# Sending the reciprocal denominators of half the heads through device memory, and folding the values in one pass

## The chip, the cores and the metric

One core of one Trainium2 chip runs the whole program. The metric is the device time of one execution in microseconds. TensorE (PE) multiplies matrices into PSUM, VectorE (DVE) and ScalarE (ACT) do elementwise work and can read PSUM, GpSimd (POOL) does elementwise work between tiles of SBUF, and SyncE (SP) here does nothing but issue DMA transfers. Each engine runs its own list of instructions in order and waits on semaphores for the others.

## The reference

The input is a batch of 32 images of 56 x 56 pixels with 32 channels. Each passes through three stages, and each stage adds to its input:

1. group norm, batch norm, a sign function, and a 3x3 convolution with binary weights;
2. layer norm and a linear attention with 16 heads of 32 columns, over the 3136 pixels of an image;
3. layer norm, and a mixture of 8 linear experts of which each token uses the best two.

The change lies in the attention. For each token `s` and head `h`, cut to what matters:

```
q = elu(x wq + b) + 1 ; k = elu(x wk + b) + 1
kv_c = sum_s k cos(s) v ,  kv_s = sum_s k sin(s) v         (32 x 32 for each head)
ksum_c = sum_s k cos(s) ,  ksum_s = sum_s k sin(s)         (32 for each head)
denom = 1 / (q cos(s) . ksum_c + q sin(s) . ksum_s + 1e-5) (one number for each token and head)
out   = (q cos(s) . kv_c + q sin(s) . kv_s) * denom, then the dense layer
```

## The kernel before

**Tiling.** An image is cut into 7 tiles of 448 tokens (4 patches of 112). The 512 columns of q are 4 chunks of 128, each with 4 heads, so `qbuf` is [128, 4 chunks, 7 tiles, 448]. Work on an image is cut into some 100 steps with two-letter names, `K0` to `K13` and so on. Those that matter here are:

- `K` (L572, L713, L991): two patches of k. PE multiplies, ACT takes the exponential (L716), DVE combines them (L994). `KX` (L578) multiplies the result by the normed input, into a bank of PSUM of its own, and `KT` (L723) copies that out once for an image. `Q` (L598, L718, L997) is the same for q, in 14 steps, without the last part.
- `G` (L589, L726), in two steps: PE multiplies `ktsb` by the folded value and output weights `p2`. ACT copies the products to `gmat` (L729) and, with 8 tiny activations of 32 x 2 elements in each step, the key sums to the diagonal blocks of `dmat` (L734), whose other elements were set to zero once (L871).
- `DN` (L604, L1003), `SU` (L615, L736): denominators of a half image (4 or 3 tiles). `RC` (L1010, L740): DVE takes the reciprocal in `den`, ACT makes its half-precision part; `RL` (L1013): DVE makes the remainder. Both parts lie in `rs`.
- `R` and `RP` (L621), 7 steps each: two matmuls with the 0/1 matrix `sel16` spread the reciprocals of a tile over the 128 partitions, for chunks 0 and 1 (`R`) or 2 and 3 (`RP`). In `R`, DVE multiplies `qbuf` by the result straight from PSUM (L1022). In `RP`, ACT copies it to `spread_r` (L751), of which there is one buffer, and POOL multiplies (L815).
- `NM` (L630, L1024): the scaled q times `gmat`, one step for each tile. `T2`, `S2`, `SM2`, `PN2`, `XH2`, `PL2`, `ZU`, `LG`, `RT`, `GT`, `F`, `OUT`: the second layer norm, the router (`RT`, L1033 to L1077), the gates, the experts and the sum.
- `SM1`, `PN1`, `XH1`, `PL1`, `CS`, `ZT`: the first layer norm and the transposes that `K` and `Q` read. `PN1` and `PN2` are a power on POOL (L793) and a product (L797).

**PSUM.** Three slots of two banks go round (the ring) among the steps in `RING`, in PE's order. PE fills a slot only when its user three steps back has been read. One bank serves the steps in `MISC` in turn. An image has 57 uses of the ring: K 14, Q 14, R 7, RP 7, F 7, G 2, ZT 2, ZU 2, LG 1, XC 1.

**Order.** `schedule()` (L137) gives each step a time by hand, in units of which 14 make a period. `SHIFTS` (L190) moves a kind of step on one engine. `iteration()` (L203) folds the times modulo 14 and sorts, so each engine works in each period on three to five images at different stages, in one fixed order. Images 3 to 28 are done by a loop whose body holds two periods (L257), the others by straight code ahead of it and after it. The times set only the order: nothing waits for a clock.

**DMA.** SP loads an image (L474, 4 transfers, at `XT`), makes four shifted copies for the convolution (L488, 4 transfers of many short rows, at `CV`), and stores the result (L493, 4 transfers, at `OUT`).

## Time and profile before

| | |
|---|---|
| time, 3 runs | median 2821.83 us (2802.16, 2821.83, 2821.9) |
| profiled execution | span 2819.6 us; the median lies 2.2 us above it |
| PE busy | 2421.4 us, 86% |
| DVE busy | 2342.6 us, 83% |
| POOL busy | 1866.9 us, 66% |
| ACT busy | 1724.8 us, 61% |
| mean granted TensorE clock | 0.929 of full speed |

A profile is one execution. The profiled execution's own time is its span and the little that lies around it (start and end of the program); the page gives the span alone. Busy time is the time in which an engine executes; time in which an instruction is blocked on a shared resource counts as busy.

### The profile page before, as it was taken

The page shows a single profiled execution, that of the slowest core. Times are in us where ns is not written, and L with a number is a line of the kernel's source. Part 1 is how long each engine was busy: PE and PEld are TensorE (multiplying, and loading weights), DVE is VectorE, ACT ScalarE, POOL GpSimd, SP SyncE. Part 2 cuts the span into 40 slices and gives each one's busy share as a digit, 9 for nine tenths or more (in the row PEclk, how much of TensorE's full clock was granted, in tenths as well). Part 3 has the DMA queues.
Part 4 walks back from the last instruction along what each step waited for, and adds up shares of the span by engine and source line. Part 5 has one row for each costly group of instructions (what it writes and reads, how often), then busy time and mean ns, then how long its engine had stood idle before and what let it go on. Part 6 is the DMA issues. An engine that isn't in the chain of part 4 may idle for free.

```text
span 2819.6 us, 56945 instructions
## 1 busy us (share of the span) xinstructions
PE 2421.4 (86%) x19300; PEld 1207.1 (43%) x19300; DVE 2342.6 (83%) x3041; ACT 1724.8 (61%) x2821; POOL 1866.9 (66%) x1479
## 2 busy tenths in 40 slices
PE   3379999898989999898999989899998989999872
PEld 3324444444444444444444444444444444444442
DVE  4457999898988889898898989888898988899873
ACT  0057766666666666666666666666666666666640
POOL 0124677777767667776776777676677767777677
PEclk7579999999999999999999999999999999999995
DMA  9100000000000000000000000000000100000000
GB/s 249 35 10 10 10 16 16 16 6 12 16 17 16 16 16 11 7 16 17 16 16 16 14 4 16 17 16 16 17 15 2 16 17 16 16 10 7 7 7 12
DMA packets 232233, 55.14 MB, mean 20 GB/s; under 512 B 226065, under 2 KB 226945, under 8 KB 231777
## 3 DMA queue, kind: packets, MB, share of 16 engines
q1 hardware_dynamic: 231904, 50.95, 9.1%
q8 instruction: 184, 3.01, 0.5%
q14 instruction: 145, 1.18, 0.1%
HBM read 31.19 MB, written 12.85 MB: 16 GB/s over the span
## 4 chain that ended last, share of the span: by engine, by line
PE 40%; DVE 22%; POOL 17%; issue 14%; ACT 3%; DMA 1%; SPq 1%; POOLq 0%; DVEq 0%; ACTq 0%
PE ps L585 10%; PE ps L576 5%; PE ps L610 5%; DVE kbuf L994 5%; POOL prod L844 5%; DVE qbuf L1000 5%; PE ps L627 4%; PE ps L636 3%; POOL prod L847 3%; DVE rs L1017 2%; DVE route L1064 2%; POOL rstd L793 2%; PE ps L601 2%; ACT ebuf L716 2%; PE ps L568 2%
## 5 line engine op out<-in xcount | busy, mean ns | idle before, releaser
L716 ACT ACTIVATE ebuf<-ps,small 112x1024 f32<-112x1024 f32 x448 | 498.6, 1113 | 384.7 <-PE ps L576 357.3
L994 DVE SCALAR_TENSOR_TENSOR kbuf<-ps,ebuf 112x1024 f32<-112x1024 f32 x448 | 546.8, 1221 | 129.4 <-ACT ebuf L716 112.0
L721 ACT ACTIVATE ebuf<-ps,small 128x896 f32<-128x896 f32 x448 | 450.1, 1005 | 317.7 <-PE ps L601 237.8
L815 POOL TENSOR_TENSOR qbuf<-spread_r,qbuf 128x896 f32<-128x896 f32 x224 | 468.2, 2090 | 141.0 <-ACT spread_r L751 140.8
L585 PE MATMUL ps<-kbuf,xcs 112*64 112x512 f32 x1792 | 506.3, 651 | 45.1 <-DVE kbuf L994 45.1
L1000 DVE SCALAR_TENSOR_TENSOR qbuf<-ps,ebuf 128x896 f32<-128x896 f32 x448 | 486.3, 1085 | 37.6 <-ACT ebuf L721 35.3
L793 POOL TENSOR_TENSOR rstd<-varr,power 112x28 f32<-112x28 f32 x64 | 307.2, 4801 | 292.7 <-DVE varr L984 290.7
L636 PE MATMUL ps<-qbuf,gmat 128*64 128x224 f32 x3584 | 403.2, 369 | 4.5 <-DVE pbuf L1028 1.7
L844 POOL TENSOR_TENSOR prod<-prod 112x512 f32<-112x512 f32 x224 | 285.3, 1274 | 159.0 <-DVE prod L1084 157.9
L1084 DVE TENSOR_TENSOR prod<-ps,gate 112x1024 f32<-112x1024 f32 x224 | 272.4, 1217 | 94.4 <-PE ps L661 79.9
L627 PE MATMUL ps<-rs,sel 128*128 128x448 f16 x896 | 249.4, 360 | 96.6 <-issue 81.7
L576 PE MATMUL ps<-wk,z 128*112 128x512 f16 x896 | 287.7, 404 | 25.5 <-DVE qbuf L1000 17.9
L636 PEld LDWEIGHTS ps<-qbuf,gmat 128*64 128x64 f32 x3584 | 243.4, 140 | 129.0 <-issue 31.8
L601 PE MATMUL ps<-z,wq 128*128 128x448 f16 x896 | 248.6, 360 | 10.3 <-DVE qbuf L1000 8.3
L1022 DVE TENSOR_TENSOR qbuf<-ps,qbuf 128x896 f32<-128x896 f32 x224 | 242.4, 1082 | 12.4 <-PE ps L627 12.1
L751 ACT ACTIVATE spread_r<-ps 128x896 f32<-128x896 f32 x224 | 205.0, 915 | 63.0 <-PE ps L627 57.9
L610 PE MATMUL ps<-qbuf,dmat 128*32 128x448 f32 x1792 | 225.5, 549 | 0.2 <-ACT mean L763 0.2
L711 ACT ACTIVATE z<-ps 128x1568 f16<-128x1568 f16 x128 | 188.4, 1472 | 12.4 <-PE ps L568 12.3
L585 PEld LDWEIGHTS ps<-kbuf,xcs 112*64 112x64 f32 x1792 | 100.7, 141 | 194.7 <-issue 126.7
L627 PEld LDWEIGHTS ps<-rs,sel 128*128 128x128 f16 x896 | 61.3, 100 | 278.3 <-issue 191.5
L576 PEld LDWEIGHTS ps<-wk,z 128*112 128x112 f16 x896 | 93.0, 131 | 193.8 <-issue 74.7
L847 POOL TENSOR_TENSOR prod<-prod 112x256 f32<-112x256 f32 x224 | 164.0, 732 | 17.6
(133 smaller groups left out, 3668.4 us busy)
## 6 DMA issues: line engine op xcount, KB each, us to landing
qbuf<-in_x SPq DMA_DIRECT2D x8, 1568.0 KB, 12.0
xt<-in_x SPq DMA_DIRECT2D x128, 98.0 KB
out<-ffn SPq DMA_DIRECT2D x128, 98.0 KB
shifted<-nat SPq DMA_DIRECT2D x128, 52.6 KB, 5.0
qbuf<-in_sel SPq DMA_DIRECT2D x1, 1024.0 KB, 11.9
tabn<-in_tabnc SPq DMA_DIRECT2D x1, 784.0 KB, 13.6
p<-in_p2c SPq DMA_DIRECT2D x1, 528.0 KB, 10.4
tabd<-in_tabdc SPq DMA_DIRECT2D x1, 448.0 KB, 11.2
```

Of the source, the lines that this page charges most:

```text
L576: mm = pe.matmul(o[0:PT, k, :], z1[:, m.par, PT * s:PT * s + PT], wk16[:, :], start=True, stop=True)
L585: mm = pe.matmul(kt_bank[64 * k:64 * k + 64, :], xcs[:, 2 * n + k, :, :].rearrange("p a c -> p (a c)"), kbuf[:, n % 2, DH * k:DH * k + DH] ...
L610: mm = pe.matmul(o[32 * j:32 * j + 32, 0:HW4], dmat[:, m.par, c, :, :].rearrange("p a h -> p (a h)"), qbuf[:, c, 4 * h + j, :], start=(c = ...
L627: mm = pe.matmul(o[:, k, 0:HW4], sel16[:, 128 * a:128 * a + 128], rs[:, j // 4, :], start=True, stop=True)
L636: mm = pe.matmul(o[64 * v:64 * v + 64, 0:2 * PT].rearrange("p (a t) -> p a t", a=2), gmat[:, m.par, c, :, :].rearrange("p a o -> p (a o)") ...
L716: act.activation(ebuf[0:PT, 0, :].rearrange("p (a b) -> p a b", a=2), o[0:PT, :, :], ACT.Exp, bias=minus_one[0:PT, :]).then_inc(kexp_made, 1)
L721: act.activation(ebuf[:, 1, 0:2 * G * PT].rearrange("p (a b) -> p a b", a=2), o[:, :, 0:G * PT], ACT.Exp, bias=minus_one).then_inc(qexp_ma ...
L793: nc.gpsimd.tensor_tensor(rstd[ln][:, :], varr[ln][:, :], power[0:PT, 0:SLOTS], ALU.pow)\
L815: nc.gpsimd.tensor_tensor(qbuf[:, 2:4, n, :], spread_r[:, :, :], qbuf[:, 2:4, n, :], ALU.mult)\
L844: nc.gpsimd.tensor_tensor(p[:, :, 0:4 * C], p[:, :, 0:4 * C], p[:, :, 4 * C:], ALU.add)\
L994: v.scalar_tensor_tensor(kbuf[:, n % 2, :].rearrange("p (a b) -> p a b", a=2), o[0:PT, :, :], 1.0, ebuf[0:PT, 0, :].rearrange("p (a b) -> ...
L1000: v.scalar_tensor_tensor(qbuf[:, k0:k0 + 2, j, :], o[:, :, 0:G * PT], 1.0, ebuf[:, 1, 0:2 * G * PT].rearrange("p (a b) -> p a b", a=2), AL ...
```

## The change

It does these things:

1. **RP leaves TensorE and ScalarE.** SP stores the reciprocals of a half image in device memory (`RC`, two transfers, semaphore `r_stored`). At each `RP` step it loads two transfers into one of now two buffers `spread_r`: four rows of 448 numbers, each written to 32 partitions. POOL waits for these instead of the ACT copy. RP is in no list of PE or ACT any more; `sel16` is halved.
2. **G is one step** and takes the bank of MISC instead of two ring slots. DVE makes the whole of `dmat` in one instruction, the key sums times a 0/1 mask; ACT then makes `gmat` in one copy. `DN0` waits for `dmat`, `NM0` for `gmat`.
3. **The order is new.** All times and shifts have new values.

The new `SP` order in a period (image counted from the one whose K steps are in the middle; from `iteration()`) is RC1/-1, RP4/-1, RP5/-1, CV/+2, RP6/-1, OUT/-3, RC0/0, RP0/0, RP1/0, RP2/0, XT/+3, RP3/0; before it was CV/+1, OUT/-3, XT/+3.

```diff
-    dsum = dsum.astype(np.float32)
+    heads = np.kron(np.eye(HEADS).reshape(CH, HPC, 1, HEADS).transpose(1, 0, 2, 3), np.ones((32, 1, 2, 1)))
+    dsum = np.concatenate([dsum, heads.reshape(128, -1)], 1).astype(np.float32)
...
+    def at_from(self, per, off, base):
+        if self.t is None:
+            return self.at(per, off)
+        return (self.t + base) * (2 * per) + (self.c * per + off - 2 * per * base)
...
-RING = ("K", "R", "RP", "Q", "G", "LG", "F", "XC", "ZT", "ZU")
-MISC = ("XT", "CV", "DN", "SU", "NM", "T2")
+RING = ("K", "R", "Q", "LG", "F", "XC", "ZT", "ZU")
+MISC = ("XT", "CV", "DN", "SU", "NM", "T2", "G")
...
-    add("SM1", [-7.96])
-    add("PN1", [-9.24])
+    add("SM1", [-11.55])
...
-    add("ZT", [-5.63, -1.39])
+    add("ZT", [-8.42, -4.05])
+    add("PL1", [-7.39])
...
-    add("RC", [12.07, 17.64])
-    add("RL", [13.24, 18.20])
-    add("R", [14.96, 15.05, 15.84, 16.71, 19.33, 20.27, 24.24])
-    add("RP", [13.85, 14.97, 15.97, 17.79, 18.78, 21.48, 23.54])
-    add("NM", [15.85, 18.60, 20.07, 20.58, 22.99, 23.72, 26.77])
+    add("RC", [9.54, 15.15])
+    add("PN1", [9.97])
+    add("RL", [10.03, 15.51])
+    add("R", [11.18, 14.02, 14.07, 14.40, 17.49, 18.01, 21.23])
+    add("RP", [12.27, 12.36, 12.81, 15.35, 16.76, 17.88, 22.82])
+    add("NM", [13.90, 16.08, 17.97, 18.30, 20.08, 21.27, 24.17])
...
-    "gpsimd": {"F": -2.19, "RP": -1.61, "T2": -1.77},
-    "sync": {"CV": 5.7, "OUT": 3.11, "XT": -9.83},
+    "gpsimd": {"CS": 2.47, "F": 0.75, "GT": -14.35, "OUT": 1.00, "PL1": -3.59, "PL2": 2.79, "PN1": -23.18,
+               "PN2": 1.57, "RP": -0.97, "T2": 0.32},
+    "sync": {"CV": -8.67, "OUT": 6.28, "RC": -0.55, "RP": -1.98, "XT": -5.25},
...
-        spread_r = sb("spread_r", [128, 2, HW4])
+        spread_r = sb("spread_r", [128, 2, 2, HW4])
+        r_rows = nc.dram_tensor("r_rows", [2, HEADS, TILES * HW4], F32).ap()
...
+                if kind == "RC":
+                    w = HALF[n]
+                    rows = r_rows[m.par].rearrange("h (j c t) -> c j h t", j=TILES, c=2)[:, 4 * n:4 * n + w]
+                    sp.wait_ge(recip_made, m.at(2, n + 1))
+                    for c in range(2):
+                        sp.dma_start(rows[c], den[64 * c:64 * c + 16 * w, 0:HALFW]).then_inc(r_stored, 16)
+                if kind == "RP":
+                    sp.wait_ge(r_stored, m.at(64, 32 * (n // 4) + 32))
+                    wait(sp, qp_made, m.at_from(7, n - 1, 7 * m.par + n + 1))
+                    for k in range(2):
+                        heads = r_rows[m.par, 8 + 4 * k:12 + 4 * k, HW4 * n:HW4 * (n + 1)]
+                        sp.dma_start(spread_r[:, (7 * m.c + n) % 2, k, :],
+                                     heads.unsqueeze(1).to_broadcast([4, 32, HW4])).then_inc(r_spread[(7 * m.c + n) % 2], 16)
...
                 elif kind == "G":
-                    act.wait_ge(ring_full, no + 1)
-                    src = o[:, :, 0:66].rearrange("p k (a o) -> p k a o", a=2)
-                    act.activation(gmat[:, m.par, 2 * n:2 * n + 2, :, :], src[:, :, :, 0:C], ACT.Copy)
-                    for h in range(HPC):
-                        q = slice(32 * h, 32 * h + 32)
-                        for k in range(2):
-                            c = 2 * n + k
-                            last = act.activation(dmat[q, m.par, c, :, HPC * c + h], src[q, k, :, C], ACT.Copy)
-                    last.then_inc(g_made, 1)
+                    act.wait_ge(dmat_made, m.at(1, 1))
+                    act.activation(gmat[:, m.par, :, :, :].rearrange("p c a o -> p (c a) o"),
+                                   o[:, 0:264].rearrange("p (k o) -> p k o", o=33)[:, :, 0:C], ACT.Copy)\
+                        .then_inc(g_made, 1)
                 elif kind == "SU":
                     act.wait_ge(misc_full, no + 1)
                     wait(act, r_made, m.at(2, n))
+                    wait(act, r_stored, m.at(64, 32 * n))
...
-                elif kind == "RP":
-                    act.wait_ge(ring_full, no + 1)
-                    wait(act, qp_made, m.at(7, n))
-                    act.activation(spread_r[:, :, :], o[:, :, 0:HW4], ACT.Copy).then_inc(r_copied, 1)
...
                 elif kind == "RP":
-                    pool.wait_ge(r_copied, m.at(7, n + 1))
-                    nc.gpsimd.tensor_tensor(qbuf[:, 2:4, n, :], spread_r[:, :, :], qbuf[:, 2:4, n, :], ALU.mult)\
+                    slot = (7 * m.c + n) % 2
+                    t0 = 0 if m.t is None else m.t
+                    pool.wait_ge(r_spread[slot], t0 * 224 + 32 * ((7 * m.c + n) // 2 + 1))
+                    nc.gpsimd.tensor_tensor(qbuf[:, 2:4, n, :], spread_r[:, slot, :, :], qbuf[:, 2:4, n, :], ALU.mult)\
                         .then_inc(qp_made, 1)
...
+                elif kind == "G":
+                    dve.wait_ge(misc_full, no + 1)
+                    ksum = o[:, 0:264].rearrange("p (k o) -> p k o", o=33)[:, :, C:C + 1].to_broadcast([128, 8, HEADS])
+                    v.tensor_tensor(dmat[:, m.par, :, :, :].rearrange("p c a h -> p (c a) h"), ksum,
+                                    dsum_sb[:, 64:].rearrange("p (k h) -> p k h", k=2 * CH), ALU.mult)\
+                        .then_inc(dmat_made, 1)
```

## Rows read from the trace of the kernel before

**Rows 1.** The page, busy time of each engine, and the clock in 40 slices.

```profile
PE 2421.4 (86%) x19300; PEld 1207.1 (43%) x19300; DVE 2342.6 (83%) x3041; ACT 1724.8 (61%) x2821; POOL 1866.9 (66%) x1479
PEclk7579999999999999999999999999999999999995
```

**Rows 2.** One line's instructions: the copy KT, once for each image.

```profile
L725 ACT ACTIVATE ktsb<-ps x32: 587/597/598, 194.1 to 2680.5; 128x512 f32<-128x512 f32 x32
```

**Rows 3.** Windows: length, busy PE, PEld, DVE, ACT, POOL, clock, DMA share, GB/s.

```profile
1022.41:1101.23 78.82, 72.44 (x599) 35.45 (x601) 71.79 (x90) 53.59 (x88) 58.03 (x46) 0.98 0.08 14
1101.23:1186.27 85.04, 75.89 (x598) 37.19 (x601) 71.78 (x90) 53.70 (x88) 58.35 (x48) 0.92 0.08 14
```

**Rows 4.** Timeline of PE: start, length, what, idle before it and what ended it.

```profile
1065.25 0.44 PE L594 MATMUL ps<-p,ktsb 128*32 128x66 f32 x16 [2.31 <-DVE qbuf L1000]
...
1106.77 1.08 PE L585 MATMUL ps<-kbuf,xcs 112*64 112x512 f32 x4
...
1113.50 0.54 PE L627 MATMUL ps<-rs,sel 128*128 128x448 f16 x2 [1.51 <-issue]
1114.58 1.03 PE L576 MATMUL ps<-wk,z 128*112 128x512 f16 x2 [0.54 <-DVE qbuf L1000]
...
1116.29 1.96 PE L585 MATMUL ps<-kbuf,xcs 112*64 112x512 f32 x4
```

**Rows 5.** Timeline of PE where the loop turns.

```profile
1007.77 1.97 PE L585 MATMUL ps<-kbuf,xcs 112*64 112x512 f32 x4 [3.15 <-DVE kbuf L994]
```

**Rows 6.** Windows of 4 us in both places, columns as in rows 3.

```profile
1113.00:1117.00 4.00, 2.96 (x10) 1.46 (x12) 2.16 (x5) 2.24 (x3) 2.00 (x2) 0.71 0.00 0
1007.00:1011.00 4.00, 3.23 (x10) 1.35 (x11) 0.09 (x1) 0.47 (x1) 1.79 (x1) 0.50 0.03 6
```

**Rows 7.** What DVE waited for from 1022.41 to 1101.23: us, times, longest.

```profile
DVE kbuf L994 <- ACT ebuf L716: 2.4, 3, 1.5
DVE nat L963 <- PE ps L543: 1.6, 1, 1.6
...
DVE kbuf L994 <- PE ps L585: 0.4, 1, 0.4
```

**Rows 8.** Chain of waits, an RP step of PE: start, length, what.

```profile
1099.29 0.48 PE ps L627 x2
```

**Rows 9.** Groups of instructions by line: busy us, mean ns, idle before, releaser.

```profile
L815 POOL TENSOR_TENSOR qbuf<-spread_r,qbuf 128x896 f32<-128x896 f32 x224 | 468.2, 2090 | 141.0 <-ACT spread_r L751 140.8
L751 ACT ACTIVATE spread_r<-ps 128x896 f32<-128x896 f32 x224 | 205.0, 915 | 63.0 <-PE ps L627 57.9 <-POOL qbuf L815 4.2
L1017 DVE TENSOR_TENSOR rs<-den,r_high 64x224 f16<-64x224 f32 x128 | 141.7, 1107 | 6.5 <-ACT r_high L743 3.7
L1028 DVE TENSOR_TENSOR pbuf<-ps,tabn 128x224 f32<-128x224 f32 x224 | 86.0, 384 | 23.4 <-PE ps L636 21.2
```

**Rows 10.** Two lines of DVE: ns of one, shortest, median, longest; first and last start.

```profile
L1064 DVE TENSOR_TENSOR route<-route,rmax x32: 391/3327/3335, 326.1 to 2787.9; 112x224 f32<-112x224 f32 x32
L1017 DVE TENSOR_TENSOR rs<-den,r_high x128: 384/821/2578, 213.2 to 2724.0; 64x224 f16<-64x224 f32 x128
```

**Rows 11.** Timeline of DVE and of POOL at one place.

```profile
1136.04 3.33 DVE L1064 TENSOR_TENSOR route<-route,rmax 112x224 f32<-112x224 f32 x1
...
1126.87 4.80 POOL L793 TENSOR_TENSOR rstd<-varr,power 112x28 f32<-112x28 f32 x1 [7.59 <-DVE varr L984]
...
1137.03 2.10 POOL L815 TENSOR_TENSOR qbuf<-spread_r,qbuf 128x896 f32<-128x896 f32 x1
```

**Rows 12.** DMA issues: what, queue, KB each, median us from issue to landing.

```profile
shifted<-nat SPq DMA_DIRECT2D x128, 52.6 KB, 5.0
...
qbuf<-in_conv_rows SPq DMA_DIRECT2D x1, 144.0 KB, 2.2
...
mean_sb<-in_mean SPq DMA_DIRECT2D x1, 64.0 KB, 1.8
```

**Rows 13.** SP's instructions of one line: ns, shortest, median, longest.

```profile
L488 SPq DMA_DIRECT2D shifted<-nat x128: 591/664/1383, 113.4 to 2515.6; - x128
```

More of the change, by code:

```diff
@@ L170, in schedule @@
-    add("TB", [15.28])
-    add("T2", [21.90, 24.63, 24.96, 27.84])
-    add("S2", [24.40, 27.26, 27.43, 29.55])
-    add("SM2", [29.73])
-    add("PN2", [27.61])
-    add("XH2", [31.86])
-    add("PL2", [30.69])
-    add("ZU", [33.29, 33.68])
-    add("LG", [34.09])
-    add("RT", [34.52, 34.80, 35.84, 36.19, 36.22, 36.95, 37.18])
-    add("GT", [35.17])
-    add("F", [37.89, 38.65, 39.01, 39.68, 40.71, 42.71, 44.87])
-    add("OUT", [46.76])
+    add("XT", [-25.28, -24.71])
+    add("CV", [-15.38, -14.76])
@@ new lines, in schedule @@
+    add("XC", [-12.33])
+    add("CS", [-11.62, -3.29])
+    add("SM1", [-11.55])
+    add("XH1", [-9.82])
+    add("ZT", [-8.42, -4.05])
+    add("PL1", [-7.39])
+    add("K", [-5.99, -4.61, -4.18, -3.48, -1.29, -0.10, 0.21, 0.99, 1.50, 2.59, 2.95, 3.66, 3.98, 4.64])
+    add("KX", [-4.41, -3.31, -2.10, -1.29, 0.17, 1.03, 1.61, 2.88, 2.96, 3.50, 3.83, 4.61, 5.49, 6.00])
+    add("Q", [1.30, 2.72, 3.57, 3.87, 4.45, 4.87, 5.71, 6.66, 8.41, 8.66, 9.55, 11.62, 12.64, 13.40])
+    add("TB", [3.59])
@@ L185, in schedule @@
+    add("PL2", [22.76])
+    add("PN2", [23.76])
+    add("XH2", [24.42])
+    add("SM2", [26.29])
+    add("ZU", [31.31, 31.79])
+    add("RT", [31.88, 32.01, 32.35, 32.38, 32.61, 32.74, 33.95])
+    add("LG", [32.03])
+    add("F", [35.71, 35.77, 36.26, 36.56, 38.49, 40.45, 42.65])
+    add("OUT", [42.57])
+    add("GT", [48.88])
     return sorted(s)
@@ L279, in build @@
         pair_sb = sb("pair_sb", [128, 66])
-        dsum_sb = sb("dsum_sb", [128, 64])
+        dsum_sb = sb("dsum_sb", [128, 64 + 2 * CH * HEADS])
         eye16 = sb("eye16", [128, 128], F16)
-        sel16 = sb("sel16", [128, CH * G * 128], F16)
+        sel16 = sb("sel16", [128, CH // 2 * G * 128], F16)
         p2 = sb("p2", [128, CH, 2, HPC, 33])
@@ L403, in build @@
         g_made = sem("g_made")
+        dmat_made = sem("dmat_made")
         den_made = sem("den_made")
@@ L409, in build @@
         qr_made = sem("qr_made")
-        r_copied = sem("r_copied")
+        r_stored = sem("r_stored")
+        r_spread = [sem(f"r_spread{k}") for k in range(2)]
         qp_made = sem("qp_made")
@@ L456, in _ @@
                              (tabd[:, :, :].rearrange("p a b -> p (a b)"), tabdc), (tabk[:, :, :].rearrange("p a b -> p (a b)"), tabkc),
-                             (first[:, :], firstc), (views["sel"], sel),
+                             (first[:, :], firstc), (views["sel"], sel[:, 0:CH // 2 * 4 * 128]),
                              (tabn[:, :, :].rearrange("p a b -> p (a b)"), tabnc)):
@@ L590, in step @@
                     pe.wait_ge(kt_copied, m.at(1, 1))
-                    for k in range(2):
+                    for c in range(CH):
                         for h in range(HPC):
-                            a = HPC * (2 * n + k) + h
-                            mm = pe.matmul(o[32 * h:32 * h + 32, k, 0:66].rearrange("p (a o) -> p a o", a=2),
-                                           ktsb[:, 32 * a:32 * a + 32], p2[:, 2 * n + k, :, h, :],
+                            a = HPC * c + h
+                            mm = pe.matmul(o[32 * h:32 * h + 32, 66 * c:66 * c + 66].rearrange("p (a o) -> p a o", a=2),
+                                           ktsb[:, 32 * a:32 * a + 32], p2[:, c, :, h, :],
                                            start=True, stop=True)
-                    mm.then_inc(ring_full, 1)
+                    mm.then_inc(misc_full, 1)
                 elif kind == "Q":
@@ L617, in step @@
                     for c in range(2):
-                        mm = pe.matmul(o[64 * c:64 * c + 64, 0:HALFW], dsum_sb[:, :],
+                        mm = pe.matmul(o[64 * c:64 * c + 64, 0:HALFW], dsum_sb[:, 0:64],
                                        dcs[:, HALFW * c:HALFW * (c + 1)], start=True, stop=True)
                     mm.then_inc(misc_full, 1)
-                elif kind in ("R", "RP"):
-                    j, k0 = n, 2 if kind == "RP" else 0
+                elif kind == "R":
+                    j, k0 = n, 0
                     pe.wait_ge(r_made, m.at(2, 1 + j // 4))
@@ L870, in _ @@
             v.memset(nat[:, :, :], 1.0)
-            v.memset(dmat[:, :, :, :, :], 0.0)
             for ln in range(2):
```

32 lines of the change are left out of this document (11 added, 21 removed), and 5 rows, old and new, of the table SHIFTS.

## The prediction

> **What bounds the kernel now.** I read the page first. PE is busy 86% and DVE 83% of the span, and the slices show both level from the fourth on, with a clock near full [rows 1]. So the middle decides, and I count it by images. The copy KT runs once for an image, 31 intervals between 194.1 and 2680.5 us, so an image takes (2680.5 - 194.1)/31 = 80.2 us [rows 2]. Ahead of the first KT lie 194 us, behind the last 139.
>
> Windows cut at the same step two images apart show the shape of a loop turn: one image of 78.82 us and one of 85.04 [rows 3]. In the short one DVE is busy 71.79 us and PE 72.44; neither alone fills it. It is a queue of three slots between them that keeps both at 91%. POOL (58.0) and ACT (53.6) have some 20 us and more to spare.
>
> The timeline of PE tells what breaks its 72 us. (a) `G` waits 2.31 us for a ring slot that DVE has not read yet [rows 4]. (b) The `RP` matmul that follows the second `SU` too closely waits 1.51 us for the reciprocals' remainder. The step behind waits 0.54, and then PE runs slowly: `K` takes 1.03 us, `KX` 1.96 against 1.08 a few us before [rows 4]. The granted clock there is 0.71 over 4 us, between the two levels of 2.4 and 1.2 GHz, right behind an idle PE [rows 6]. (c) Where the loop turns PE is idle 3.15 us and then the clock is at 0.50, the lower level [rows 5, 6]; that is the long image's extra 6.2 us.
>
> DVE's busy time is not all work. The router's product L1064 takes 3.33 us, but 0.39 where it takes least [rows 10]; at the place shown it ends 0.24 us after a POOL product has [rows 11]. The remainder L1017 has 384 ns as shortest and 1107 as mean [rows 9, 10]. Both read two SBUF tiles while POOL runs.
>
> **The change, part by part.** Each for one image.
>
> *RP off PE.* A step holds PE's path 0.48 us in the chain [rows 8]; seven are 3.4 us. *The wait (b).* The new order has thirteen PE steps between SU1 and the next step that needs the reciprocals, R4; before there were seven. 1.51 + 0.54 idle go, and with them the slow stretch: 0.9 us on `KX` alone, with `K` and its neighbour some 1.6. PE's busy 72.4 becomes 72.4 - 3.4 - 1.6 = 67.4 us. PE is then no longer near its bound.
>
> *RP off ACT.* 7 x 0.915 = 6.4 us [rows 9] and the 16 tiny activations leave an engine with over 20 us to spare. Worth nothing by itself; if the exponentials came late it would show as DVE waiting for ACT, 2.4 us of which are there now [rows 7], one third from a late copy at most.
>
> *G.* Two ring uses and seven RP uses go: 57 become 48, so each slot has a fifth more time. Wait (a) goes from G, but the slot was late because DVE was, and DVE's work stays. I give nothing for it. DVE takes on the mask product, 128 x 128 elements from PSUM: more than nothing, at most the 0.384 us of L1028 with 224 [rows 9]. I take 0.3, near the upper end. It stands in the path, since DN0 waits for it.
>
> *POOL* keeps its seven products of 2.09 us [rows 9], the same bytes from the same kind of tile. Before, they waited for the ACT copy, 141 us in all. Now they wait for DMA.
>
> *The transfers.* SP takes on 4 stores and 14 loads. By the cost of its `CV` issues, 0.66 us each [rows 13], that is at most 12 us of its 78; its old 12 issues stay. The store of RC (56 KB) lands in about 1.8 us, the time of a 64 KB load [rows 12]. No row shows a load that repeats its rows. Lower end: the two single loads of 64 and 144 KB give 0.005 us a KB over a fixed 1.5 us [rows 12], so a pair of 224 KB each lands 3.7 us after issue. Upper end: a quarter of that rate, as four source rows might be served by four queues' worth of engines, gives 1.5 + 2 x 4.5 = 10.4 us. The schedule sets SP's RP 1.01 units ahead of POOL's, and a unit is 78.8/14 = 5.6 us. At 3.7 the load is hidden behind POOL's other work; I take this end, since the single loads are the rows nearest in form.
> In SP's queue, RP6 now stands behind the shifted copies (5.0 us to land [rows 12]) and RP3 behind an image load, RC0 behind OUT. The shifted copies wait for the binarized image of two ahead, long before RP6 is wanted; I cost this at nothing, and 5 us once an image if the cover is gone.
> The clearing of `dmat`, the smaller `sel16`, the larger mask: under 1 us once. The new lead-in and tail I take as unchanged, 10 us either way.
>
> *The sum.* With PE at 67.4 us, DVE sets the pace. Its 7.0 us of idle time in the short image (78.82 - 71.79) shrink by what PE's lateness caused: the wait for `XT` behind the slow stretch, 1.6, about 0.8 of the 2.4 for the exponentials [rows 7], and 0.4 in a `K` behind the slow `KX` [rows 7]: 2.8. Added work 0.3. The image takes 78.8 - 2.8 + 0.3 = 76.3, a gain of 2.5; the turn of the loop stays, since the body still holds two periods. 31 x 2.5 = 78 us: the span goes from 2819.6 to 2742, and the time, 2 us above it, to 2744. The median was 2.2 us above the profiled span, so both may be set against each other.
>
> **The rivals.**
>
> *1. DVE is freed too.* The blocked time is 3.33 - 0.39 = 2.9 us for L1064 and 4 x (1.107 - 0.384) = 2.9 for the four L1017 of an image. In the new order RL1 comes when POOL is near its wait for the norm's row sums, where it idles 7.59 us now [rows 11]. If half of the 5.8 goes, 31 x 2.9 = 91 us more: about 2653. Against it: RT2 comes some way behind PN1, when POOL has a row of products without a gap.
>
> *2. The gain is eaten.* The same blocking, the other way: POOL's power takes 4.80 us [rows 11], and one more DVE product meeting it costs up to 4.4. Where DVE sets the pace, 2.5 us lost this way leave the time as it was, 2820. Or the 7 us of DVE idle time simply move: the slots have more time, but the order was not the only cause.
>
> *3. Slower: the spread loads come late.* If the broadcast of four rows goes at a quarter of the rate, a pair lands after 10.4 us, 4.7 later than the schedule's 5.7. There are two buffers, so a load can't be issued before the product two steps back. POOL works in order: RP2 late makes CS1, F5, RP3, PN1, then PL1 and the next image's ZT late, and PE waits. POOL is busy 58.0 and waits 7.6 for row sums. With three late loads it needs 58.0 + 7.6 + 14.1 = 79.7, and half a loop turn of 6.2 makes 82.8: 0.9 over the 81.9 of now. With four, 5.6 over. It decides from the third late load on. 0.9 gives 2850, and between three and four 2880 is a fair figure. For it: the source's outer dimension has length 4 in the code. Against: 20 us of POOL's idle time, and RP4 to RP6 have much slack.
> The Trainium skill, "DMA: Bandwidth & Descriptors", section "Why a DMA increments its semaphore by 16 and not by 1", says that a transfer uses as many engines, up to 16, as divide the slowest dimension of both sides. It would put these loads on four engines. No run here has shown it yet.
>
> *4. The change doesn't do what it says*, for instance POOL goes on waiting for a late reciprocal as before: PE's 3.4 us alone, 76 to 79 us an image. This lies in the cases above.
>
> **How the numbers follow.** A measurement of this kernel can tell about 1%, 28 us, from no change (one of the three runs lay 0.7% below the others). My forecast has 0.50, its own range 2700 to 2790 (1.0 to 3.9 us an image). Rival 1 has 0.12 (2640 to 2700), rival 2 0.20 (2790 to 2850), rival 3 0.18 (above 2850). The predicted time is 2744. The range from 2680 to 2850 leaves out most of rival 1 and rival 3. Faster by over 1%: 0.50 + 0.12 = 0.62; within 1%: 0.20; slower: 0.18.
>
> **What would show it.** KT intervals of 76 us in short images and still some 6 more in long ones. No PE wait after SU1, and no slow `KX` there. PE busy under 68 us an image, DVE 72 and the least idle. POOL's waits for the spread loads below 3 us an image. A pair landing in over 6 us, with POOL idle ahead of L815 and PE waiting for ZT or NM, would show rival 3; L1064 and L1017 at their shortest, rival 1; PE and DVE both idle with no late engine named, rival 2. The forecast is wrong if DVE's idle time doesn't fall though PE's busy time does.

## The result, and the profile after

The changed kernel is slower: 2879.81 us (median of 4 runs, 2874.01 to 2887.52) against 2816.86 (median of 4, 2802.16 to 2821.9). The ratio is 1.022, with a 95% interval of 1.0181 to 1.0259. The forecast was 2744. The profiled execution took 2887.52 us with a span of 2885.7, so the profile shows the longest of the four runs, 0.3% above the median.

From the page, busy time of each engine, its share and instructions, then the clock in 40 slices:

```profile
PE 2405.2 (83%) x18852; PEld 1177.2 (41%) x18852; DVE 2264.4 (78%) x3072; ACT 1496.9 (52%) x2053; POOL 1860.3 (64%) x1479
PEclk7589999898999999999999989989999999999995
```

Against [rows 1] the work did shrink: DVE 78 us less, ACT 228 us less, PE 16 us less. The time grew all the same, so the loss is in waits and in a slower PE. The copy KT has line 745 now:

```profile
L745 ACT ACTIVATE ktsb<-ps x32: 589/589/607, 185.7 to 2752.7; 128x512 f32<-128x512 f32 x32
```

An image takes (2752.7 - 185.7)/31 = 82.8 us, against 80.2 in [rows 2]: 31 x 2.6 = 81 us more. The stretch before the first KT is 8 us shorter and the one after the last 6 us shorter. Two windows that together make one turn of the loop (length, then busy PE, PEld, DVE, ACT, POOL, clock, DMA share, GB/s), to be set beside [rows 3]:

```profile
1022.82:1111.22 88.40, 75.06 (x583) 35.30 (x581) 67.85 (x92) 46.41 (x65) 58.08 (x46) 0.90 0.20 52
1111.22:1192.50 81.28, 73.19 (x591) 34.94 (x588) 70.86 (x93) 47.26 (x65) 57.88 (x46) 0.96 0.22 56
```

Both images are longer, the long one by 3.4 and the short one by 2.5 us. (A turn of the loop is some 4 us longer than two images of the mean, before as after: 163.9 against 160.4 and 169.7 against 165.6.) DVE has less to do in both, and is idle for 20.6 and 10.4 us where it was 13.3 and 7.0.

What the engines waited for: engine, line and its release, us in total, times, longest:

```profile
POOL qbuf L829 <- DMA spread_r<-r_rows: 193.1, 45, 27.7
...
DVE pbuf L1047 <- PE ps L656: 158.5, 65, 6.7
...
PE ps L656 <- POOL qbuf L829: 105.8, 34, 7.5
```

This is a chain of three. POOL's product of the second half of the heads (`RP`, L829, before L815) waits for a spread load. PE's `NM` (L656) waits for POOL. DVE's part of `NM` (L1047) waits for PE. The 34 waits of PE are about one for an image. Their place is `NM0`, the first of seven. The same chain in time, first SP's queue (start and length, what, how many):

```profile
1018.90 1.19 SPq L499 DMA_DIRECT2D r_rows<-den  x2
1023.53 11.38 SPq L505 DMA_DIRECT2D spread_r<-r_rows  x6
...
1107.62 1.19 SPq L499 DMA_DIRECT2D r_rows<-den  x2
1111.22 11.59 SPq L505 DMA_DIRECT2D spread_r<-r_rows  x6
```

POOL, with the idle time before the instruction and what ended it in brackets:

```profile
1031.75 2.08 POOL L829 TENSOR_TENSOR qbuf<-spread_r,qbuf 128x896 f32<-128x896 f32 x1 [4.58 <-DMA spread_r<-r_rows]
...
1119.65 2.08 POOL L829 TENSOR_TENSOR qbuf<-spread_r,qbuf 128x896 f32<-128x896 f32 x1 [3.76 <-DMA spread_r<-r_rows]
```

The store of RC0 is issued at 1018.90, the first load can be issued 4.63 us later, and POOL starts 8.22 us after that. In the next image it is 3.60 and 8.43 us. So POOL begins `RP0` 12 to 13 us after the reciprocals' store is issued. PE at the same place:

```profile
1033.97 3.25 PE L656 MATMUL ps<-qbuf,gmat 128*64 128x224 f32 x16 [3.29 <-POOL qbuf L829]
...
1044.63 1.10 PE L594 MATMUL ps<-wk,z 128*112 128x512 f16 x2 [3.18 <-DVE kbuf L1007]
1045.65 3.21 PE L628 MATMUL ps<-qbuf,dmat 128*32 128x448 f32 x12
...
1121.88 2.73 PE L656 MATMUL ps<-qbuf,gmat 128*64 128x224 f32 x16 [2.48 <-POOL qbuf L829]
...
1127.62 1.70 PE L628 MATMUL ps<-qbuf,dmat 128*32 128x448 f32 x12
```

PE is idle for 3.29 and 2.48 us. Then it is slow: `NM0` takes 3.25 and 2.73 us, where the one without a wait in the experiments below takes 1.7. Over the 26 images of the loop the waits are 2.48 to 3.40 us, 78 us together, and `NM0` takes 29 us more than 26 times 1.73. In the first image the denominators (`L628`), behind the turn of the loop, are slow too, 3.21 us against 1.70 for the same twelve matmuls one image later.

```profile
1034.00:1037.00 3.00, 3.00 (x16) 1.84 (x16) 0.00 (x0) 1.11 (x1) 3.00 (x1) 0.50 0.31 101
1045.60:1048.60 3.00, 3.00 (x13) 0.58 (x12) 2.12 (x2) 1.95 (x2) 0.73 (x1) 0.50 0.25 82
```

That is two windows, columns as above, over the slow `NM0` and the slow denominators. The granted clock is 0.50 in both, the lower of the two levels (1.2 GHz), right behind an idle PE. The length of the wait doesn't settle it: in four of the 26 images `NM0` takes 1.73 or 1.74 us behind waits of 2.84 to 3.25 us. DVE (columns as for PE) shows the turn of the loop:

```profile
1037.26 0.39 DVE L1047 TENSOR_TENSOR pbuf<-ps,tabn 128x224 f32<-128x224 f32 x1 [4.67 <-PE ps L656]
1043.27 1.22 DVE L1007 SCALAR_TENSOR_TENSOR kbuf<-ps,ebuf 112x1024 f32<-112x1024 f32 x1 [5.62 <-issue]
```

Behind its part of `NM0` DVE reaches the end of the loop's body and waits there 5.62 us for nothing that the profile shows. Whether the late loads cause this is asked below, in the run with idle transfers.

### The profile page after: what moved, and what is told of

It reads as the page before. It is cut to its first block, busy times and chain, and to the rows that moved or that the text cites. A ratio compares the mean times of both kernels' runs of the same rounds, so it can differ in the third digit from the quotient of the medians.

```text
span 2885.7 us, 55585 instructions
## 1 busy us (share of the span) xinstructions
PE 2405.2 (83%) x18852; PEld 1177.2 (41%) x18852; DVE 2264.4 (78%) x3072; ACT 1496.9 (52%) x2053; POOL 1860.3 (64%) x1479
## 4 chain that ended last, share of the span: by engine, by line
PE 31%; issue 25%; DVE 20%; POOL 16%; ACT 4%; DMA 3%; DVEq 1%; POOLq 1%; SPq 0%; ACTq 0%
PE ps L656 7%; POOL prod L858 6%; PE ps L603 5%; PE ps L628 5%; DVE kbuf L1007 4%; POOL prod L861 4%; DVE qbuf L1013 3%; PE ps L594 3%; POOL qbuf L829 2%; PE ps L619 2%; PE ps L645 2%; DVE nat L976 2%; DVE route L1078 2%; DMA qbuf<-in_x 2%; DVE qbuf L1041 2%
## 5 line engine op out<-in xcount | busy, mean ns | idle before, releaser
L829 POOL TENSOR_TENSOR qbuf<-spread_r,qbuf 128x896 f32<-128x896 f32 x224 | 467.6, 2093 | 193.1 <-DMA spread_r<-r_rows 193.1
L656 PE MATMUL ps<-qbuf,gmat 128*64 128x224 f32 x3584 | 427.1, 385 | 107.2 <-POOL qbuf L829 105.8
L656 PEld LDWEIGHTS ps<-qbuf,gmat 128*64 128x64 f32 x3584 | 266.4, 148 | 245.1 <-issue 153.3
L1103 DVE TENSOR_TENSOR prod<-ps,gate 112x1024 f32<-112x1024 f32 x224 | 270.5, 1219 | 43.7 <-POOL ffn L864 30.2
L619 PE MATMUL ps<-z,wq 128*128 128x448 f16 x896 | 254.9, 367 | 13.5 <-DVE kbuf L1007 12.4
L834 POOL TENSOR_TENSOR xc<-t,mean 112x256 f32<-112x256 f32 (+1 forms) x128 | 72.2, 574 | 299.3 <-ACT mean L775 299.3
L628 PE MATMUL ps<-qbuf,dmat 128*32 128x448 f32 x1792 | 247.2, 578 | 0.2 <-ACT mean L775 0.2
L586 PE MATMUL ps<-eye,parts 112*64 112x112 f16 (+1 forms) x3840 | 133.5, 222 | 96.2 <-DVE qbuf L1013 52.5
L1047 DVE TENSOR_TENSOR pbuf<-ps,tabn 128x224 f32<-128x224 f32 x224 | 86.5, 386 | 159.6 <-PE ps L656 158.5
L861 POOL TENSOR_TENSOR prod<-prod 112x256 f32<-112x256 f32 x224 | 163.9, 732 | 17.6
L586 PEld LDWEIGHTS ps<-eye,parts 112*64 112x64 f16 (+1 forms) x3840 | 106.2, 112 | 166.1 <-DVE qbuf L1013 78.9
```

The lines of the kernel that those rows point to most:

```text
L619: mm = pe.matmul(o[:, k, 0:G * PT], wq16[:, 128 * (k0 + k):128 * (k0 + k) + 128], z1[:, m.par, G * PT * j:G * PT * (j + 1)], start=True, s ...
L628: mm = pe.matmul(o[32 * j:32 * j + 32, 0:HW4], dmat[:, m.par, c, :, :].rearrange("p a h -> p (a h)"), qbuf[:, c, 4 * h + j, :], start=(c = ...
L656: mm = pe.matmul(o[64 * v:64 * v + 64, 0:2 * PT].rearrange("p (a t) -> p a t", a=2), gmat[:, m.par, c, :, :].rearrange("p a o -> p (a o)") ...
L829: nc.gpsimd.tensor_tensor(qbuf[:, 2:4, n, :], spread_r[:, slot, :, :], qbuf[:, 2:4, n, :], ALU.mult)\
```

## The experiments

The ratios are to the kernel before, run on the same chip: 2821 us in each group of runs (2820.99, 2821.34, 2821.57). The changed kernel's 2879.81 is the one of the result; beside it the kernel before had 2816.86.

**No transfers.** The same kernel without SP's part.

```diff
-                if kind == "RC": ...  (the store)
-                if kind == "RP": ...  (the loads)
-                    pool.wait_ge(r_spread[slot], t0 * 224 + 32 * ((7 * m.c + n) // 2 + 1))
+                    pool.wait_ge(recip_made, m.at(2, n // 4 + 1))
```

> Leaves out: no store of the reciprocals and no spread loads; GpSimd multiplies its half of q by a fixed tile of ones, as soon as the reciprocals of the half image exist. All else is the changed kernel, its order too. Theory L (the loads land late): in the changed kernel NM0 waits 2.5 us (short image) to 3.3 us (long image) for the product behind the first load, and the slow clock behind that wait costs 1.5 to 3.5 us more; without it 4 us go from a short and 6 from a long image, 31 x 5 = 155: about 2725. Rival O (the new order itself is worse, whatever the loads do): 2850 or more.

2734.23 us, ratio 0.9704 (0.9678 to 0.973). All of the loss, and nearly the whole forecast gain, hangs on the transfers: 2880 - 2734 = 146 us.

```profile
PE 2346.6 (86%) x18852; PEld 1154.8 (42%) x18852; DVE 2295.2 (84%) x3073; ACT 1496.5 (55%) x2053; POOL 1858.9 (68%) x1479
```

An image takes 78.1 us. PE is 59 us less busy than in the changed kernel for the same 18852 instructions, at a mean granted clock of 0.936 against 0.912. DVE is 31 us busier, 21 of them at one line, the remainder `RL` (102.9 against 82.0).

**Transfers without anybody waiting.** The loads go on, POOL multiplies by a fixed row of ones, and SP issues a load when the one two steps back has landed.

```diff
-                    wait(sp, qp_made, m.at_from(7, n - 1, 7 * m.par + n + 1))
+                    wait(sp, r_spread[(7 * m.c + n) % 2], m.at_from(112, 32 * ((7 * m.c + n) // 2) - 112 * m.c, 7 * m.par + n + 1))
...
-                    pool.wait_ge(r_spread[slot], t0 * 224 + 32 * ((7 * m.c + n) // 2 + 1))
-                    nc.gpsimd.tensor_tensor(qbuf[:, 2:4, n, :], spread_r[:, slot, :, :], qbuf[:, 2:4, n, :], ALU.mult)\
+                    pool.wait_ge(recip_made, m.at(2, n // 4 + 1))
+                    nc.gpsimd.tensor_tensor(qbuf[:, 2:4, n, :], ones_r[:, :].unsqueeze(1).to_broadcast([128, 2, HW4]), qbuf[:, 2:4, n, :], ALU.mult)\
```

> Leaves out the same use, but makes all transfers: the stores and the spread loads are issued and land in the two buffers, paced by their own landing, and GpSimd multiplies by a fixed row of ones without waiting for them. Theory L: as without transfers, within 10 us (2715 to 2745). Rival C (the traffic itself costs, by delayed instruction fetches where the loop turns, 5.6 us of idle VectorE there, or by contention): 2800 or more, the loop turn's idle time as long as in the changed kernel, and shorter in the run without transfers.

2750.21 us, 0.9752 (0.9728 to 0.9776). The traffic and SP's issues cost 16 us; the other 130 of the 146 are waiting for a load. The rival's time (2800 or more) wasn't met, but its sign was: DVE's wait at the turn of the loop is as long as in the changed kernel, though nobody waits for a load.

```profile
DVE kbuf L1010 <- issue: 37.9, 7, 5.6
...
DVE kbuf L1010 <- PE ps L606: 27.0, 5, 5.7
```

That is 64.9 us over 12 turns, 5.4 each. The changed kernel has 41.4 + 30.6 us at the same instruction, 6.0 a turn; without transfers it is 35.2 us, 2.9 a turn. The slow denominators behind the turn are there too: at one turn the twelve matmuls take 3.21 us. So most of what the changed kernel loses at the turn isn't the price of a late load. It comes with these transfers, and by what path the runs don't show: with the loads of one head, the same bytes, it is 34.3 us, 2.9 a turn.

**Loads of one head.** Each load is cut in four, so that its outer dimension is 32 rows and not 4.

```diff
-                        heads = r_rows[m.par, 8 + 4 * k:12 + 4 * k, HW4 * n:HW4 * (n + 1)]
-                        sp.dma_start(spread_r[:, slot, k, :], heads.unsqueeze(1).to_broadcast([4, 32, HW4]))
+                        for h in range(4):
+                            head = r_rows[m.par, 8 + 4 * k + h:9 + 4 * k + h, HW4 * n:HW4 * (n + 1)]
+                            sp.dma_start(spread_r[32 * h:32 * h + 32, slot, k, :], head.to_broadcast([32, HW4]))
```

> Each spread load of four heads is cut into four loads of one head, a row of 448 numbers to 32 partitions. The outermost dimension is then 32 on both sides instead of 4. Nothing is left out. By the rule that a transfer is served by as many engines as divide that dimension (4 against 16), the eight loads of a tile land in some 5 to 6 us after the first issue instead of 8, SP's eight issues at 0.53 us being 4.2 us of it; the NM0 wait goes or nearly goes: 2740 to 2790 by theory L. If the loads were spread over all engines before, the landing gets later by the extra issues, and the time is 2880 or more.

2759.94 us, 0.9792 (0.9767 to 0.9816): 120 us faster than the changed kernel, with the same bytes and four times the issues. A load lands after 2.0 us, though SP's issues now take longer than the landing (a block of 24 takes 12.24 us). SP, POOL and PE at one `NM0`:

```profile
1051.42 1.26 SPq L499 DMA_DIRECT2D r_rows<-den  x2
1055.07 12.24 SPq L506 DMA_DIRECT2D spread_r<-r_rows  x24
```

```profile
1061.33 2.13 POOL L830 TENSOR_TENSOR qbuf<-spread_r,qbuf 128x896 f32<-128x896 f32 x1 [1.63 <-DMA spread_r<-r_rows]
```

```profile
1063.61 1.74 PE L657 MATMUL ps<-qbuf,gmat 128*64 128x224 f32 x16 [0.41 <-POOL qbuf L830]
```

From the first issue to POOL's start it is now 6.26 us. That is eight issues (about 4 us, by 12.24/24 = 0.51 each) and one landing of about 2. `NM0` waits 0.41 us and keeps its full speed.

**Loads of two heads.** The same cut in halves, outer dimension 2.

```diff
+                        for h in (0, 2):
+                            heads = r_rows[m.par, 8 + 4 * k + h:10 + 4 * k + h, HW4 * n:HW4 * (n + 1)]
+                            sp.dma_start(spread_r[32 * h:32 * h + 64, (7 * m.c + n) % 2, k, :],
+                                         heads.unsqueeze(1).to_broadcast([2, 32, HW4])).then_inc(r_spread[(7 * m.c + n) % 2], 16)
```

> The changed kernel with each load of four heads cut into two loads of two heads; outermost dimension 2. A control for the loads of one head: same bytes, more and smaller transfers. If the number of engines follows the outermost dimension, these go by 2 engines: a tile takes some 13 us instead of 8, seven tiles 91 us, more than an image's time, so DMA sets the pace: over 3000. If smaller transfers as such were what made the one-head loads land soon, it lies between 2760 and 2880.

3439.83 us, 1.22 (1.2148 to 1.2252).

```profile
POOL qbuf L830 <- DMA spread_r<-r_rows: 942.1, 189, 32.1
```

POOL starts three products in a row at 1013.12, 1022.91 and 1032.12 us, 9 to 10 us apart. The smaller piece with the smaller outer dimension is the slower one. Bytes and number of transfers can't explain the three cuts, 2 (3440 us), 4 (2880) and 32 (2760); the outer dimension orders them.

The windows show it directly. The column before the last is the mean busy share of the core's 16 DMA engines. Three stretches of 3 us with spread loads under way and no other transfer, in the changed kernel (outer dimension 4), here (2) and in the run with four copies below (16):

```profile
1116.00:1119.00 3.00, 2.76 (x13) 0.87 (x12) 3.00 (x5) 2.22 (x3) 0.00 (x0) 1.00 0.25 86
```

```profile
1105.00:1108.00 3.00, 3.00 (x16) 1.05 (x13) 2.88 (x6) 2.01 (x2) 0.45 (x1) 1.00 0.13 42
```

```profile
1058.00:1061.00 3.00, 3.00 (x18) 1.38 (x18) 3.00 (x4) 2.26 (x5) 2.18 (x3) 1.00 0.71 220
```

Four of 16 engines that are always busy would give a share of 0.25, two of them 0.13 (the view doesn't tell the engines apart). The GB/s go with it: 86, 42, 220.

**A flat store on top of that.** Beside the loads of one head, device memory is laid out so that the store too has one long outer dimension (64 or 48 rows) in place of 4 or 3 times 16.

```diff
-        r_rows = nc.dram_tensor("r_rows", [2, HEADS, TILES * HW4], F32).ap()
+        r_rows = nc.dram_tensor("r_rows", [2, TILES * HEADS, HW4], F32).ap()
...
-                    rows = r_rows[m.par].rearrange("h (j c t) -> c j h t", j=TILES, c=2)[:, 4 * n:4 * n + w]
+                    rows = r_rows[m.par].rearrange("r (c t) -> c r t", c=2)[:, 64 * n:64 * n + 16 * w]
```

> One-head loads, and the reciprocals lie in device memory by tile, then head, so that a store's rows form one dimension of 64 (or 48) instead of 4 (or 3) by 16. Theory L: the store, 3.65 us from issue to the first load's issue, lands about 1.5 us sooner, and what is left of POOL's wait at RP0 (1.6 us at one place seen) goes: 2740 to 2755. If the store's time is latency and not engines, as before: 2760.

2746.21 us, 0.9745 (0.9694 to 0.9796). This computes the whole reference and is the best version found, 2.5% below the kernel before and 12 us above the one without transfers.

```profile
1049.35 1.15 SPq L499 DMA_DIRECT2D r_rows<-den  x2
1052.06 12.20 SPq L506 DMA_DIRECT2D spread_r<-r_rows  x24
```

POOL starts `RP0` at 1057.86, after 0.25 us of waiting for the load. Its waits over the whole run:

```profile
POOL qbuf L830 <- DMA spread_r<-r_rows: 43.7, 15, 23.9
```

From the store's issue to the first load's it is 2.71 us, in the next image too, where it was 3.65 and 4.49 with the loads alone cut. POOL has 15 waits left, and 23.9 of the 43.7 us are one of them. The two intervals touch, so the 14 us between this run and the one before are likely, not certain.

**Four copies in memory.** The flat store writes each row four times, and a load takes 16 rows, each to 8 partitions: two loads a tile again, outer dimension 16.

```diff
+        r_rows = nc.dram_tensor("r_rows", [2, TILES * HEADS, 4, HW4], F32).ap()
...
+                        sp.dma_start(rows[c], den[64 * c:64 * c + 16 * w, 0:HALFW].unsqueeze(1).to_broadcast([16 * w, 4, HALFW])).then_inc(r_stored, 16)
...
+                        heads = r_rows[m.par, 16 * n + 8 + 4 * k:16 * n + 12 + 4 * k].rearrange("h q t -> (h q) t")
...
+                                     heads.unsqueeze(1).to_broadcast([16, 8, HW4])).then_inc(r_spread[(7 * m.c + n) % 2], 16)
```

> The reciprocals are stored four times over (224 KB instead of 56 a store, rows flat), and a tile's load is two transfers again, each of 16 source rows to 8 partitions; outermost dimension 16. Two issues a tile instead of eight. The first load lands some 3.5 us after its issue instead of 6.3, and the store takes 1 us longer than the flat one. Theory L: 2735 to 2750. If the fourfold store costs more than 3 us, 2760 or more.

2758.1 us, 0.9785 (0.9744 to 0.9827): a little above what was expected, and not told apart from the flat store. Landing, from the list of DMA issues (what, KB each, median us to landing):

```profile
spread_r<-r_rows SPq DMA_DIRECT2D x448, 224.0 KB, 3.3
r_rows<-den SPq DMA_DIRECT2D x64, 224.0 KB, 3.1
```

The same 224 KB to the same 128 partitions, in as many transfers as in the changed kernel, land in 3.3 us. So neither the size nor repeating rows made those slow. The price is paid in the store, whose way to the first load is 3.90 and 4.15 us in two images, against 2.71.

**The old order with everything changed.** Times and shifts of the kernel before, with RP and G placed by me.

```diff
-    add("G", [9.46, 9.86])
-    add("RP", [13.85, 14.97, 15.97, 17.79, 18.78, 21.48, 23.54])
+    add("G", [9.86])
+    add("RP", [14.6, 15.4, 16.6, 18.1, 20.3, 21.5, 23.84])
...
+    "sync": {"CV": -9.1, "OUT": 0.5, "XT": -11.0, "RC": 0.3, "RP": -1.5},
```

> The changed kernel's three code changes (RP by transfers, G in one step, two buffers) with the old kernel's times and shifts; only SP's steps, GpSimd's RP times (14.6, 15.4, 16.6, 18.1, 20.3, 21.5, 23.84) and the one G (9.86) are set anew, so that it can run. NM0 stands 3.8 units behind RC0 there against 4.4 in the new order. Theory L: NM0 waits longer than in the changed kernel, 5 us or more in each image: 2900 to 2960. Rival O: the new order was the fault, 2820 or less.

3598.18 us, 1.2763 (1.2732 to 1.2795). Every theory missed. The waits say it is my placing of POOL's products that was measured:

```profile
POOL prod L863 <- DVE prod L1108: 735.3, 153, 13.0
PE ps L661 <- POOL qbuf L834: 721.9, 158, 9.6
```

POOL waited only 160.0 us for the loads. This run says nothing of the change, only that a late product in POOL's list is dear.

**The old order without transfers.** The same, but POOL's products at the times of the kernel before, and neither store nor loads.

```diff
-    add("RP", [14.6, 15.4, 16.6, 18.1, 20.3, 21.5, 23.84])
+    add("RP", [13.85, 14.97, 15.97, 17.79, 18.78, 21.48, 23.54])
...
+    "gpsimd": {"F": -2.19, "RP": -1.61, "T2": -1.77},
...
+                    pool.wait_ge(recip_made, m.at(2, n // 4 + 1))
```

> The old order (RP of GpSimd too at its old times, waiting only for the reciprocals and multiplying by ones) with the changed kernel's code: RP in no ring slot, G in one step in the shared bank. Leaves out the spread of half the reciprocals. Beside the light RP in the old order (2829, 57 ring uses) and the new order without transfers (2734, 48 ring uses) it parts two causes. If the nine freed ring uses make the gain: 2735 to 2770. If the new order does: 2800 to 2830.

2932.25 us, 1.0391 (1.0366 to 1.0416), outside both of the ranges expected. With 48 ring uses and RP off PE and ACT it is slower than the kernel before. PE now waits for the bank that G shares, in a turn made for six kinds of steps (PE's timeline):

```profile
1009.09 3.26 PE L648 MATMUL ps<-qbuf,gmat 128*64 128x224 f32 x16 [2.93 <-DVE pbuf L1038]
...
1066.28 1.00 PE L553 MATMUL ps<-eye_center,xt 112*128 112x112 f32 x4 [5.15 <-DVE pbuf L1038]
```

These two kinds of wait come to 86.9 and 143.5 us, more than the 111 us by which the run is slower; the kernel before has 1.7 us of the first kind. So this run shows what my place of `G` costs in the old order. It doesn't part the new order from the freed ring uses, and which of the two makes the gain stays open.

**A light RP in the kernel before.** Its RP step keeps its place, but PE makes one matmul of 8 columns and ACT copies one element.

```diff
-                    for k in range(2):
+                    for k in range(2 if kind == "R" else 1):
+                        w = HW4 if kind == "R" else 8
...
-                    act.activation(spread_r[:, :, :], o[:, :, 0:HW4], ACT.Copy).then_inc(r_copied, 1)
+                    act.activation(small[:, 13:14], o[:, 0, 0:1], ACT.Copy).then_inc(r_copied, 1)
```

> The kernel before, its order and ring untouched, but RP is light: PE does one matmul of 8 columns instead of two of 448, ACT copies one element a partition, and POOL multiplies by a tile of ones once that is done. Leaves out the spread of half the reciprocals. It gives what relief of PE and ACT alone is worth in the old order. If relief is the gain, as in the prediction (PE's 3.4 us of 2.5 us an image net): 2720 to 2750. If the gain of the run without transfers (2734) needs the new order and the six freed ring uses: 2790 or more.

2828.75 us, 1.0026 (1.0008 to 1.0043): no gain. PE's busy time fell by 44 us, to 2377.2, ACT's by 162 us. Both stalls of [rows 4] stayed (PE's timeline):

```profile
1039.14 0.17 PE L628 MATMUL ps<-rs,sel 128*128 128x8 f16 x1 [1.97 <-issue]
1069.61 0.44 PE L594 MATMUL ps<-p,ktsb 128*32 128x66 f32 x16 [2.31 <-DVE qbuf L1002]
```

**R twice.** The loads of one head, and PE makes the matmuls of `R` twice.

```diff
-                    for k in range(2):
+                    for k in (0, 1, 0, 1):
```

> The one-head loads with R's two matmuls done twice into the same bank: PE gets back the time of the seven steps that the change took from it, 0.39 to 0.48 us a step, some 3 us an image, in the new order and with no ring use more. If PE's relief is part of the gain, 2760 + 31 x 3 = 2850, at least 2800. If DVE sets the pace in the new order and PE has slack, 2760 to 2780.

2778.11 us, 0.9839 (0.9816 to 0.9862). 68 us of more PE work (2345.8 to 2413.5) cost 18 us. PE has slack in the new order, but not unlimited slack.

**NM0 later.** The changed kernel, and NM0 at 14.90 in place of 13.90.

```diff
-    add("NM", [13.90, 16.08, 17.97, 18.30, 20.08, 21.27, 24.17])
+    add("NM", [14.90, 16.08, 17.97, 18.30, 20.08, 21.27, 24.17])
```

> The changed kernel, four-head loads, with one number changed: NM0 at 14.90 instead of 13.90, behind DN7 and the loop's turn. Theory L: NM0 no longer waits for the first load, whose landing is as late as before; the waits of 2.5 to 3.3 us and the slow clock go: 2760 to 2800. If the load's lateness costs through POOL (RP0 holds PN2 and the rest) and not through NM0: 2850 or more.

2808.32 us, 0.9963 (0.9934 to 0.9993): 72 us below the changed kernel. POOL waits nearly as long as ever, and much less follows from it:

```profile
POOL qbuf L829 <- DMA spread_r<-r_rows: 181.7, 47, 27.3
```

```profile
1021.55 1.74 PE L656 MATMUL ps<-qbuf,gmat 128*64 128x224 f32 x16 [1.34 <-DVE dcs L1028]
```

**The flat store, with NM0 later.** The control: loads that are in time, and the same later NM0.

> One-head loads, flat store (2746) and NM0 at 14.90. There little is left to wait for; the step only stands elsewhere: 2735 to 2755, the same within 10 us. Slower than 2760 if the new place of NM0 delays NM1 or DN4 in the one shared bank.

2774.04 us, 0.982 (0.9794 to 0.9846): 28 us above the flat store, and above the range expected. By itself the new place costs 28 us; the wait on DVE's `dcs` at the shared bank (31.2 us, 28 times) has about that size. With `NM0` at its old place late loads cost 134 us (2879.81 against 2746.21), at the later one 34 (2808.32 against 2774.04). So some 100 us hang on the wait of `NM0` for POOL's product.

## Why the prediction was wrong

**The step that failed** is the landing of the spread loads: "so a pair of 224 KB each lands 3.7 us after issue ... I take this end, since the single loads are the rows nearest in form". Measured, POOL starts 8.2 to 8.4 us after the first issue, and in the chain that ended last the loads' step is 7.50 to 7.87 us:

```profile
202.09 7.50 DMA spread_r<-r_rows
...
275.96 7.87 DMA spread_r<-r_rows
```

The range had been bounded rightly, 3.7 to 10.4, and the wrong end chosen. "Nearest in form" went by size. The loads of [rows 12] have 128 rows as outer dimension, the new ones 4, and the cuts show that this decides: 2, 4, 16 and 32 rows gave 3440, 2880, 2758 and 2760 us, and the 16-row load of the same 224 KB lands in 3.3. The busy share of the DMA engines, 0.25 with 4 rows and 0.13 with 2, is what four and two working engines of sixteen would give. The Trainium skill's rule that rival 3 named ("DMA: Bandwidth & Descriptors", "Why a DMA increments its semaphore by 16 and not by 1") agrees with all four. I gave it 0.18 because no row of before had shown it; it was the only price there was for a form that no row had.

**The slack** was misread as well, but by the sum below this alone would have cost nothing. I set 3.7 against the 5.7 us that lie between SP's RP and POOL's RP. But `RP0` can't be issued at its place in the order: it waits for the store, whose issue the reciprocals themselves release, and that is 4.6 or 3.6 us more. I priced the store (1.8 us) and then left it out of the sum. What counts is store plus load, 12.85 and 12.03 us in the two images. Without the waits of 3.29 and 2.48 us, 9.56 and 9.55 of them would have been in time for `NM0`. With 3.7 for the load in place of 8.2 to 8.4 the two would have come to 8.3 and 7.3.

**Where it shows.** Rival 3's time, 2850 to 2880, was met, but not by its path; that the time agrees is luck. It expected RP2 to delay POOL's chain to PL1 and the next `ZT`, from the third late load on. The runs with NM0 moved show some 100 us on `RP0` to `NM0`, one late load for an image. The timelines say the same: over the 26 images of the loop, 78 us of waiting and 29 of slower `NM0`. In one turn of the loop from above that is PE idle 3.29 + 2.48 us and `NM0` slower by 1.52 and 1.00 (against 1.73), 8.3 us. The interval of KT is 82.8 us in the changed kernel, 78.8 with idle transfers and 78.1 without any. Two images are thus 8.1 us longer than with idle transfers, where nobody waits, and those are 1.3 us longer than two without transfers. DVE's longer wait at the turn and the slow denominators behind it belong to these 1.3, since the run with idle transfers has them.

**PE's relief** (-3.4 and -1.6 us an image). The forecast was that PE drops to 67.4 us an image, 5.0 less. Without transfers it is (2421.4 - 2346.6)/32 = 2.3 less. A step of RP holds 0.48 us of the chain [rows 8], but the light RP shows only 44/32 = 1.4 us of busy time an image for seven (at a lower granted clock, 0.916 against 0.929), and R twice shows 68/32 = 2.1. In the old order this relief bought nothing.

**ACT and G at nothing**: right. 162 us less of ACT in the light RP gave nothing, and the 2.31 us stall of G didn't move, so DVE was the late one as the prediction said. The mask product was put at 0.3 us and has 281 ns:

```profile
L1019 DVE TENSOR_TENSOR dmat<-ps,dsum_sb 128x128 f32<-128x128 f32 x32 | 9.0, 281 | 0.2 <-PE ps L612 0.2
```

**The wait (b)** after SU1 is gone, with the slow `KX` behind it: right at that place. In the changed kernel and in the one without transfers no step of PE waits for the reciprocals' remainder behind an `SU`. The light RP, which kept the old order, kept the wait; so it was the order that took it away. But the slow stretch came back elsewhere, and this is a part of why PE's relief fell short. Without transfers PE waits for DVE's `Q` once in most images (52.3 us, 28 times):

```profile
1023.24 1.38 PE L573 MATMUL ps<-eye,parts 112*32 112x112 f16 x30 [1.91 <-DVE qbuf L999]
...
1027.87 1.97 PE L590 MATMUL ps<-kbuf,xcs 112*64 112x512 f32 x4
```

The granted clock from 1026.00 to 1029.60 is 0.50, and `KX` (`L590`) takes 1.97 us again.

**DVE sets the pace, 2.5 us an image**: the sum without transfers was nearly right, 2734 against 2744, by partly other terms. Measured against before it is 80.2 - 78.1 = 2.1 us an image. DVE's idle time fell by (477.0 - 436.5)/32 = 1.3 us, half of the 2.8 forecast, and its busy time by 47/32 = 1.5 where 0.3 more was forecast. The rest of the gain lies in the ends, which I had taken as unchanged: 31 x 2.1 = 64 us of the span's 88 come from the images, 24 from the stretches ahead of the first KT (9) and behind the last (15). That 2734 and 2744 lie so close is partly luck.

**Rival 1, DVE freed**: its two lines did gain, and two others paid it back. The lines of before and their like without transfers (busy us, mean ns):

```profile
L1055 DVE TENSOR_TENSOR route<-route,rmax 112x224 f32<-112x224 f32 x64 | 31.7, 495 | 2.2
L1059 DVE TENSOR_TENSOR route<-route,first 112x224 f32<-112x224 f32 x64 | 24.8, 387 | 1.1
...
L1064 DVE TENSOR_TENSOR route<-route,rmax 112x224 f32<-112x224 f32 x32 | 99.0, 3092 | 0.1
```

```profile
L1022 DVE TENSOR_TENSOR rs<-den,r_high 64x224 f16<-64x224 f32 x128 | 102.9, 804 | 3.3 <-ACT r_high L745 0.5
...
L1060 DVE TENSOR_TENSOR route<-route,rmax 112x224 f32<-112x224 f32 x64 | 70.7, 1104 | 2.2
L1064 DVE TENSOR_TENSOR route<-route,first 112x224 f32<-112x224 f32 x64 | 66.5, 1039 | 0.1
...
L1069 DVE TENSOR_TENSOR route<-route,rmax 112x224 f32<-112x224 f32 x32 | 20.0, 626 | 0.1
```

L1064 fell from 99.0 to 20.0 us and L1017 [rows 9] from 141.7 to 102.9, 118 us together. The two products ahead of it rose by 39.0 and 41.7. That leaves 37 of the 47 us by which DVE's busy time fell. (L1055 and L1059 answer to L1060 and L1064 in the second fence, L1064 to L1069, L1017 to L1022.)

**Open**: how the 16 us of idle traffic arise (DVE's wait at the turn is 2.5 us longer there, some 30 us over 12 turns, of which a part is made up elsewhere; the shifted copies land in 6.0 us, 5.1 with loads of one head and 5.0 before), and why the turn is longer with these transfers; whether the gain without transfers comes from the new order or from the freed ring slots; whether four copies are worse than the flat store at all.
